# Layer zero's front rebuilt by batch: one add-minimum per score tile, the gate in the value weights, batch one's router and scatters under batch two's attention

## The reference

```python
h = _layernorm(x) * (1 + ca) + sa
x = x + ga * _L0_attn_ref(h, Wq, bq, Wk, bk, Wv, bv)   # one causal head of width 128
h = _layernorm(x) * (1 + cb) + sb
x = x + gb * _L0_ffn_ref(h, router_w, w1, b1, w2, b2)  # 8 experts, top 1, capacity 384
# layer 1: the same with 16 heads and relative position bias, then LoRA experts, top 2
```

## Time and profile before

| | us |
|---|---|
| median of 3 runs | 1002.38 |
| profiled execution | 1003.77 |
| its span | 1002.0 |
| TensorE, matmuls busy | 907.5 (91%) |
| VectorE busy | 607.9 (61%) |
| ScalarE busy | 645.6 (64%) |
| POOL busy | 272.4 (27%) |

### The profile page before, as it was taken

One profiled execution on the slowest core, in us unless ns is written; L12 is line 12 of the kernel. 1 busy time (PEld: TensorE's weight loads), 2 busy tenths in 40 slices (PEclk: granted clock), 3 DMA queues, 4 the chain that ended last, 5 costly groups with the idle time before them and its releaser, 6 DMA issues. The chain is left out here.

```text
span 1002.0 us, 25392 instructions
## 1 busy us (share of the span) xinstructions
PE 907.5 (91%) x10220; PEld 666.4 (67%) x10220; DVE 607.9 (61%) x1369; ACT 645.6 (64%) x1101; POOL 272.4 (27%) x328
## 2 busy tenths in 40 slices
PE   7888619836999999999999999999999999998987
PEld 5566517714677777776777777677776777776776
DVE  5266601157566666666666666666675666667975
ACT  2544204316787787778878778778878877885343
POOL 1100360050332413233142332423234142214110
PEclk8899859957999999999999999999999999999999
DMA  8300322110002000200200100020020002000000
GB/s 258 123 1 2 158 65 65 48 42 1 2 1 89 2 2 2 89 1 3 89 2 2 72 18 2 2 89 2 2 89 2 2 2 39 2 2 2 1 16 27
DMA packets 27128, 35.48 MB, mean 35 GB/s; under 512 B 6042, under 2 KB 21716, under 8 KB 26836
## 3 DMA queue, kind: packets, MB, share of 16 engines
q1 hardware_dynamic: 25988, 31.76, 9.5%
q0 software_dynamic: 1024, 2.10, 0.7%
HBM read 28.48 MB, written 5.37 MB: 34 GB/s over the span
## 5 line engine op out<-in xcount | busy, mean ns | idle before, releaser
L533 DVE CUSTOM_DVE_ANT_0 soft<-SC,strips 128x1024 f32<-128x1024 f32 x256 | 303.3, 1222 | 79.0 <-PE SC L375 78.9
L494 ACT ACTIVATE soft<-soft,nmax 128x1024 f32<-128x1024 f32 x256 | 294.0, 1149 | 3.6 <-DVE nmax L533 3.6
L411 PE MATMUL CX<-PTs,V 128*64 128x256 f32 x2048 | 244.7, 381 | 0.0
L479 ACT COPY PTs<-PT 128x1024 f32<-128x1024 f32 x128 | 129.6, 1013 | 138.5 <-PE PT L394 138.5
L375 PE MATMUL SC<-qk 64*128 64x512 f32 x1536 | 212.1, 408 | 7.3 <-DVE nmax L533 7.0
L394 PEld LDWEIGHTS PT<-ident,soft 64*128 64x128 f32 x4096 | 158.9, 139 | 70.0 <-issue 34.8
L411 PEld LDWEIGHTS CX<-PTs,V 128*64 128x64 f32 x2048 | 142.7, 137 | 92.7 <-issue 35.0
L541 DVE COPY PTs<-PT 128x512 f32<-128x512 f32 x128 | 88.5, 692 | 161.0 <-PE PT L394 161.0
L394 PE MATMUL PT<-ident,soft 64*128 64x64 f32 x4096 | 176.3, 226 | 3.7 <-ACT PTs L486 2.4
L375 PEld LDWEIGHTS SC<-qk 64*128 64x128 f32 x1536 | 137.2, 188 | 32.8 <-issue 5.2
L322 POOL CAST qk<-raw_qk 128x512 fp32r<-128x512 f32 x60 | 36.8, 613 | 260.2 <-ACT raw_qk L298 260.2
(11 more groups left out here) (242 smaller groups left out, 1008.9 us busy)
## 6 DMA issues: line engine op xcount, KB each, us to landing
strips<-bias_vec SPq DMA_DIRECT2D x8, 1920.0 KB, 6.9
arena<-in_L_ffn_w SPq DMA_DIRECT2D x1, 2048.0 KB, 10.0
slots_in<-arena SPq DMA_DIRECT2D x1, 1536.0 KB, 9.0
arena<-slots_in SPq DMA_DIRECT2D x8, 192.0 KB, 3.6
slots_out<-arena SPq DMA_DIRECT2D x8, 192.0 KB, 2.0
x<-in_L_attn_x SPq DMA_DIRECT2D x2, 512.0 KB, 4.9
out<-x SPq DMA_DIRECT2D x4, 256.0 KB, 2.3
arena<-in_L_wmod SPq DMA_DIRECT2D x2, 384.0 KB, 5.5
```

Source lines behind the costliest of these rows:

```text
L411: ins = pe.matmul(CX[hd * DK:(hd + 1) * DK, 0:2 * P], V1[:, vb, t, hd * DK:(hd + 1) * DK], PTs[:, g % 2, hd, t, :], start=(t == 0), stop=( ...
L479: act.copy(turned_out(n, 0), turned_in(0)).then_inc(ev("ptA_out"), 1)
L494: act.activation(soft[:, n % RING, hd, :], soft[:, n % RING, hd, :], ACT.Exp, bias=nmax[:, j:j + 1], scale=-1.0, accum_out=rsum[:, hd, n % ...
L533: dve.tensor_tensor_reduce(soft[:, n % RING, hd, :], SC[hd][:, :], strips[:, u // B % 2, hd, i * P:i * P + S], 1.0, 3.4e38, ALU.add, ALU.m ...
```

## The change

- x of batch one is loaded first, x of batch two after the weights. wmod of layer one is used late, under the scatters; Wo and the first pair weights are loaded early.
- Square roots of layer zero's norms give way to an inverse root in 11 small operations (VectorE) or 14 (POOL). Rows of the norms go to `rows0`.
- The first attention starts with batch one alone; norm and fills of batch two stand in slots 2 and 3 of it. Batch two's tiles run from the widest down. Four buffers hold exponentials.
- q carries -QK_SCALE, so one operation adds the mask and takes the minimum, and the exponential no longer reads the score bank. ScalarE copies all transposes.
- ga is multiplied into Wv and bv by POOL; the context then needs one operation.
- Batch one's second norm, router, ranks and scatters stand in and under batch two's attention. Ranks start from a base per expert; logits are chosen from directly.
- The bias vector is made after batch two's logits, and so the strips are loaded after that. Thirty keep-clock products stand ahead of the wait for the scatters, none behind it.

```diff
@@ block.sync
+sp.dma_start(x[:, tiles(0), :], ...)          # first; then the 8 rows, Wq Wk Wv, wmod[0], x of batch two, bv, Wo
+load_weights(sp, 0)                           # ahead of the wait for vec_ready
@@ block.gpsimd
+            pool.wait_ge(ev("mod_copied"), 2)
+            gate(0, 0, rows_mod)
+            pool.wait_ge(ev("w0T_ready"), 1)
+            pool.wait_ge(ev("ld_bv"), 16)
+            pool.tensor_tensor(w0v, bc_tiles(w0T[:, 2, :], B), mod[:, 0, :, 0, :], ALU.mult)
+            pool.tensor_tensor(bvg, bc_tiles(bvb, B), mod[:, 0, :, 0, :], ALU.mult).then_inc(ev("gate0_folded"), 1)
+            gate(0, 3, rows_mod)
...
+            pool.wait_ge(ev("var_ready"), batches_until(1, 0))
+            inverse_roots(tiles(0))
+            pool.wait_ge(ev("h_ready"), 6)
+            link(pool.tensor_tensor(rows_mod[:, tiles(0), :], rows0[:, tiles(0), :], bc_tiles(mod[:, 0, 0, 2, :], TB), ALU.mult))
+            link(pool.tensor_tensor(rows_mod[:, tiles(0), :], rows_mod[:, tiles(0), :], bc_tiles(mod[:, 0, 0, 1, :], TB), ALU.add))
+            pool.wait_ge(ev("slots_zeroed"), 16)
+            scatter(0)                        # waits for slot_numbers 1, issues 8
+            pool.wait_ge(ev("rows_mod_ready"), 1)
+            scatter(1)                        # waits for slot_numbers 2, issues 8
+            pool.wait_ge(ev("mod_copied"), 4)
+            gate(1, 0, tmp[:, 24:30, :])
...
@@ block.scalar
+            def exp0(i):
+                act.wait_ge(ev("nmax0"), i + 1)
+                row = exps0[i % 4][:, 0:width0(i)]
+                act.activation(row, row, ACT.Exp, bias=nmax[:, i % 4:i % 4 + 1], scale=-1.0,
+                               accum_out=rsum[:, 0, i % 8:i % 8 + 1]).then_inc(ev("exp0"), 1)
...
+                if i == 2:
+                    norm_out(0, (1,))
+                if i == 3:
+                    fills_out(1)
+                if i == 14:
+                    norm_out(1, (0,))
@@ block.vector
+            def biased0(i):
+                w = width0(i)
+                dve.wait_ge(ev("scores0"), i + 1)
+                if i >= 4:
+                    dve.wait_ge(ev("pt0_full"), i - 3)
+                dve.tensor_tensor_reduce(exps0[i % 4][:, 0:w], scores_bank0(i)[:, 0:w], mask0[:, S - w:S], 1.0, 3.4e38,
+                                         ALU.add, ALU.min, nmax[:, i % 4:i % 4 + 1]).then_inc(ev("nmax0"), 1)
...
+                if i == 12:
+                    dve.wait_ge(ev("inverse_ready"), 1)
+                    rows_out(tiles(0), rows0)
+            stats0(NT - 4)
+            router_choice(0)
+            added0(NT - 3)
+            stats0(NT - 3)
+            added0(NT - 2)
+            stats0(NT - 2)
+            slot_places(0)
+            added0(NT - 1)
+            stats0(NT - 1)
+            dve.wait_ge(ev("var_ready"), batches_until(1, 1))
+            inverse_roots(tiles(1))
+            rows_out(tiles(1), rows0)
...                                            # modulated rows of batch two, 2 products
+            router_choice(1)
+            slot_places(1)
@@ block.tensor
+            def fill(f):
...
+                if kind == "v":
+                    pe.wait_ge(ev("gate0_folded"), 1)
+            for f in range(5):
+                fill(f)
             for i in range(NT + 3):
+                if i < NT: scores0(i)
+                if i == 1: fill(5)
+                if 2 <= i < NT + 2: turn0(i - 2)
+                if i >= 3: context0(i - 3)
+                if i == 2:
+                    pe.wait_ge(ev("v0_out"), 2)
+                    turn_rows(0, 2)
+                    turn_rows(0, 3)
+                if i == 3:
+                    for f in range(6, 12):
+                        fill(f)
+                if i == 13: turn_rows(1, 0); turn_rows(1, 1)
+                if i == 15: logits0(0)
+                if i == 17: ranks0(0)
+            keep_clock(PT[0], 14)
+            turn_rows(1, 2)
+            keep_clock(PT[0], 2)
+            turn_rows(1, 3)
+            keep_clock(PT[0], 3)
+            logits0(1)
+            bias_columns(0)
+            bias_columns(1)
+            ranks0(1)
+            bias_columns(2)
+            bias_columns(3)
+            mod_rows(1)
+            pe.wait_ge(ev("vec_ready"), 1)
+            keep_clock(PT[0], 30)
             pe.wait_ge(ev("scattered"), 16 * NT)
-            keep_clock(four_sc[3], 8)
```

More of the change, by code:

```diff
@@ L89, in build @@
         x = sb("x", [P, NT, D])
+        with nc.sbuf_tensor("rows_mod", [P, NT, D], F32) as rows_mod:
+            pass
         masked = sb("masked", [P, 2, 2, 512], F32R)
@@ L108, in build @@
         wo_out = sb("wo_out", [P, 2, 2, 2, D])
+        with nc.sbuf_tensor("first", [P, 4, S], F32) as first:
+            pass
         qk0 = sb("qk0", [P, 4, S], F32R)
@@ L925, in norm_stats, with inverse_roots @@
                     norm_variance(n, b)
+            def inverse_roots(some):
+                var, half, y, t = st[:, 2, some], st[:, 3, some], st[:, 5, some], st[:, 4, some]
+                link(ts(y.bitcast(I32), var.bitcast(I32), -0.5, 1597463007.0, ALU.mult, ALU.add))
+                link(ts(half, var, -0.5, None, ALU.mult))
+                for _ in range(3):
+                    link(tt(t, y, y, ALU.mult))
+                    link(tt(t, t, half, ALU.mult))
+                    link(dve.scalar_tensor_tensor(out=y, in0=t, scalar=1.5, in1=y, op0=ALU.add, op1=ALU.mult))
@@ new lines, in rows_out, with silu @@
+            def rows_out(some, h=h):
+                for t in range(some.start, some.stop):
+                    ins = ts(h[:, t, :], x[:, t, :], mv[:, t, 0:1], st[:, 5, t:t + 1], ALU.subtract, ALU.mult)
+                    if t % 4 == 3:
+                        ins.then_inc(ev("h_ready"), 1)
+            def silu():
+                dve.wait_ge(ev("silu_exp"), 1)
+                link(ts(siluT, siluT, 1.0, None, ALU.add))
+                link(dve.reciprocal(siluT, siluT))
+                tt(siluT, siluT, cols[:, C_C:C_C + 4], ALU.mult).then_inc(ev("silu_ready"), 1)
+                ts(cols[:, C_BQS:C_BQS + 1], cols[:, C_BQ:C_BQ + 1], -QK_SCALE, None, ALU.mult).then_inc(ev("bq_scaled"), 1)
```

608 lines of the change are left out of this document (327 added, 281 removed).

## The result

The changed kernel took 973.64 us (median of 4 runs, 970.86 to 975.01) against 1002.08 us for the kernel before beside it (four runs, three of them those behind the 1002.38 of the start): ratio 0.971 (0.966 to 0.976), 28.4 us less. The forecast was 965, with a range of 954 to 978. The profiled execution took 973.75 us (span 972.0).

The account below looks back on a forecast made before the run. Four stages in sequence fill the first 146.9 us, ahead of an unchanged 855 us chain. Terms -24.2 + 4.3 - 10.9 - 10.3 + 1.2 + 2.5 = -37.4 gave 965 us against the 1002.38 median, range 954 to 978.

Parts of the forecast that it names:

- Start: Stage up to the first score matmul: from 47.65 to about 23.5 us (22.3 to 26), 24.2 us earlier.
- Attention: First attention, first score to last add: from 54.0 to about 58.3 us, bounds 53 and 63.
- Norm and router of batch two: Last add to batch two's first scatter: from 23.8 to 12.9 us.
- Scatters: Scatter stage until the slots are reloaded: from 21.5 to 11.2 us, batch one's eight done at +9.8.
- Strips: Two strip loads now overlapping last scatters and first slot load: 1.2 us lost, between no cost and 5.
- Experts cold: Expert stage starts at 1.2 GHz after about 9 us of idle TensorE: 2.5 us lost (0 to 3).
- Behind the gathering: Stretch from the first gather behind the experts to the end: predicted unchanged at 802.6 us.
- (1): Rival: batch one's scatters under VectorE's norm of batch two are blocked on POOL, total 970; chance 0.12.
- (2): Rival: the moved fills serialize the attention to 63 to 66 us, total 972; chance 0.17.
- (3): Rival: full clock at the start, fills in gaps (attention 53), no strip or clock loss, total 955; chance 0.12.
- (4): Rival: the clock never rises in the expert stage, whose work doubles, total 1006; chance 0.01.
- (5): Rival: batch one's places are late, all scatters shift behind batch two's, up to +10, total 975; chance 0.06.

Follow-up runs that it names:

- e3: Changed kernel with the gate left out of the value weights, VectorE multiplying by it per tile: 965.02 us, ratio 0.9673 to the kernel before.
- b1: Kernel before with only the scaled q, one add-minimum per score tile and four exponential buffers: 994.35 us, ratio 0.9982.
- e4: Changed kernel with POOL's second gate (expert stage's output) moved behind batch two's scatters: 971.63 us, ratio 0.9700 to the kernel before.
- e1: Changed kernel with the two strip loads issued behind the eight slot loads: 960.83 us, ratio 0.9642 to the kernel before.
- e6: Changed kernel with 14 more keep-clock products before turning batch two's rows and 16 before the reloaded slots' turning: 971.80 us, ratio 0.9707 to the kernel before.
- c1: Changed kernel with strip loads behind the slot loads and the second gate behind batch two's scatters: 966.44 us, ratio 0.9630 to the kernel before.
- c2: Changed kernel with strip loads behind the slot loads and batch one's scatters held until batch two's places exist: 980.34 us, ratio 0.9766 to the kernel before.
- c4: Changed kernel with strips and second gate late, ranks before bias columns, 28 keep-clock products before turning rows, gate unfolded: 966.16 us, ratio 0.9638 to the kernel before.
- c3: Changed kernel with strips and second gate late, ranks before bias columns, 28 keep-clock products before turning batch two's rows: 968.96 us, ratio 0.9658 to the kernel before.

## Why the prediction was right or wrong

The direction and 27 to 31 of 37.4 us came as forecast, and the range held. The shortfall of 6.6 to 7.4 us of span is a sum with both signs: a shorter attention and expert stage hide part of what the norm, the strips and the stretch behind the gathering cost more. By its steps:

- **Start.** Right in one profile (23.05), 2.6 us short in the other (26.15). The order of events is as predicted: x at 4.9, the v fill waiting for POOL. Two sizes were off. "less for a comparison": on 256 columns a comparison took 0.85 to 0.87 us and a product 0.72, so the gate and its folding took 6.45 us (15.19 to 21.64) and not 5.2. And TensorE, idle for the 3 us of that wait, ran the fills behind it at half clock. "it waits for the folded gate" was right, and e3 prices it: 4.7 to 5.0 us of the start.
- **Attention.** 56.7 and 57.2 for 58.3. With b1's 50.2 as the first part both parts are near (50.9 and 7.4 predicted), though b1 is only an approximation of that part. An unforeseen loss in it was the 1.1 to 1.5 us by which POOL's second gate delayed the first add-minimum (e4); 0.6 to 1.0 of it showed in the attention's length.
- **Norm and router of batch two.** This step failed, by 3.6 and 6.1 us. Rows at +5.8 came true (+5.77: 88.66 in the first profile). From there "transposes, hT and eight logits to +8.5" was 2.7 us; VectorE read the logits at +11.9 and +12.15, 6.1 and 6.4 us behind the rows, and 4.6 in the best profile (e1). Even with the clock up the chain to their modelled end is 3.5 us (e6), and what holds the reader beyond it is open. The second part is "the bias columns end before the one-hot and cost nothing at full clock, 1.7 at the low one": the low clock came in the second profile, TensorE being idle for 3.8 us ahead of the stage, and cost 2.33 us of waiting; in the first it was 0.16.
- **Scatters.** The split works: batch one's eight issues took 0.96 us each (the first 1.24) at a pitch of 1.264 under VectorE's work (a product of 1024 columns included) and were done at +10.5, against +9.8. c1 and c2 price the split at 10.4 us, the sum had 10.3. That holds with the strips out of the way; beside them the split was worth 4 to 5 us by the medians.
- **Strips.** This term was mis-sized: 1.2 us for what measures 4.4 (2.93 at the last scatter's landing, 1.45 at the first slot's) and, with the experts that start cold behind it, 5.6; 7 to 9 by the medians. The overlap in the prediction was right (strips from about +17 to +27; in the trace +21 to +31, as late as the places were), and it named "5 if scatters and slots both suffer". I chose near the wrong end: DMA was at 0.75 of its time through this whole stage.
- **Experts cold.** 1.3 us for 2.5 (4.08 against 2.82 for the first four products). TensorE idled 3.9 us ahead of the slots, not the 9 that the prediction had.
- **Behind the gathering**, +1.5 to +2.1 us that I had at nothing. In the changed kernel TensorE's clock was 0.51 from 203 to 217 us, while layer one's first units ran. But the stretch behind the gathering ran from 798.1 to 805.0 us over all profiles, more by group than by edit, so that a cost of the change is not shown here.

Of the rivals, (1) did not happen: the scatters were not stretched in either profile of the changed kernel. (2) did not: 57 and not 63 to 66. (3) did not: the attention was 4 us above its 53, and the strips cost. (4) did not: the clock was 0.50 from 119 to 121 us, 0.91 in the next two and 1.00 from 123 on. (5) did not: the first scatter follows the last add by 0.37 us, as predicted. None of the rivals had the loss that occurred, strips against scatters and slots together.

The rule of the Trainium skill, "SBUF — State Buffer", section "A bandwidth-pool intuition that's wrong (but worth ruling out)", gives 620 ns for a DMA issued by POOL alone and 3100 ns beside a VectorE copy. The prediction had made that a factor of five for all of VectorE's work, but batch one's scatters run beside small operations, rows and products, and no such copy. Here the sixteen issues took 0.95 to 0.97 us, and 1.24 for the first, beside VectorE or not; the longest of all in the other profiles were 1.00 and 1.08 us (e3) and 1.12 (c4). For ordinary operations a loss showed in the other direction: VectorE's eight rows took 3.87 us beside POOL's gate and 2.13 without, and 2.30 beside the gate's comparisons alone (e3).

## What to carry to other kernels

When a queue's work is moved earlier, list what transfers are in flight at its new end: here the split scatters were worth 10 us with the queue free and 4 to 5 in the way of loads that nobody needed yet, and swapping two blocks on the issuing queue gave 0.7 to 0.9% back. In this kernel the stage behind an idle TensorE came at half clock in half of the profiles: so whatever stands ahead of the one needed result on TensorE's queue should be priced at twice its length too. Don't count on dummy products to win it back: with the clock held at 1.00, VectorE read the logits no earlier. And such products are work like any other once the queue behind them is ready: in c3 and c4 they held the slots back by some 4 us, an estimate from 6.6 and 6.8 us against e1's 2.5. Last, read a mark together with the next ones before an edit is given credit for it.

## What the runs showed that I had not expected

- The landing of the last scatter took 1.3 us with the queues empty and 4.3 to 5.2 us beside two loads of 1920 KB.
- POOL on 128x256: a comparison with a constant 0.85 us, a product of two tiles 0.72; it was the shorter kind that stretched VectorE's rows.
- Two profiles of the same kernel differed by 3.1 us in the first score. The weights for q, k and v were turned at 8.96 in one and at 7.63 in the other; 0.2 us of the difference was left when batch two's scatters started.
